# One product per tile for v and the router, selection in two halves, and written-out routed turns on TensorE: an attention block with routed experts on one core

## The chip, the cores and the metric

The kernel runs on one NeuronCore of a Trainium2 chip. The metric is the device time of one execution in microseconds. Every figure of the kernel before comes from one profiled execution of 688.34 us; three timed runs gave 687.27, 690.47 (the median) and 694.31 us. In the profile PE is TensorE (PEld its weight loads, PEldq its sequencer's own register and wait instructions), DVE is VectorE, ACT is ScalarE, POOL is GpSimd and SP is SyncE, which only issues DMAs here; a q behind an engine's name is its queue of such issues.

## The reference, cut to what matters

B=8 sequences of S=256 tokens with E=256 features, so T=2048 tokens or NT=16 tiles of 128.

```python
xn = layernorm(x)
# attention: 16 heads of 16, rope on q and k, causal
q, k, v = xn @ Wq + bq, xn @ Wk + bk, xn @ Wv + bv
attn = softmax(causal(rope(q) @ rope(k).T / sqrt(16))) @ v @ Wo + bo
# feed-forward: 64 experts of width 176, top 6 of a softmax, 2 shared experts
scores = softmax(xn @ gate_w.T)
topk_w, topk_ids = top_k(scores, 6)
topk_w = topk_w / (sum(topk_w) + 1e-20)
routed = sum over the six of topk_w * (silu(g) * u) @ w_down.T
shared = (silu(sg) * su) @ ws_down.T
return x + attn + routed + shared
```

## The kernel before, in words

The program is one block in which each engine has its own list of instructions and meets the others at semaphores (`then_inc` raises one, `wait_ge` waits for it). There are four stages, in this order on TensorE.

**Prologue.** DVE normalises the 16 tiles in four groups of 2, 2, 4 and 8 (`layernorm`, L700 to L719): statistics, an ACT square root (L537), two Newton steps, then one L718 per tile. TensorE begins with 20 idle products (`WARM`, L1022), then turns each tile over (`xn_transpose`, L1009), ACT copies it to `xnT` (L527), TensorE multiplies it by the 64 router columns (`route`, L1017), and ACT copies the logits (L532). The v products come apart from that, two tiles to a product (L1040): two of them after tile 3, two after tile 7, four among the q and k products. q and k are 16 products of 512 tokens (L1035), evacuated by ACT (L545). Meanwhile DVE picks the six experts of each token (L737 to L760) over all 16 tiles in one go: softmax, the eight largest (`max`), a mask of what lies above the sixth, and a scan that settles ties. TensorE waits for it at L1078, forms ranks from triangular products (L1083, L1084) and sends counts to DVE, which works out each slot's row and the tables of experts (L770 to L813). `tables_ok` lets TensorE go on into the shared experts.

**Shared experts** (32 tiles, L1148 to L1186), with DVE listing tokens beside them.

**Routed experts.** 128 tiles of 128 rows, each of two strips of 64 rows that may belong to different experts. Two tiles make a turn. In a turn TensorE does, in order: two `x_transpose` (L1135) of tiles four ahead, two `h_transpose` (L1171), two `up` (L1162) of tiles two ahead, two `down` (L1204). The first strip's weights are taken from a ring of eight experts at an address that is computed from a register; the second strip's weights are copied by DVE to a fixed place (`up_copy` L882, `down_copy` L888; `gu_own` and `dn_own` tell TensorE). After each `down` TensorE loads the expert number of the tile four ahead from the table in SBUF into a register (`load_expert`, L1111, a TENSOR_LOAD; DVE has its own, L872). All engines but POOL run most of the turns in a hardware loop of two turns (`eng.Fori`, L308), so the semaphore counts they wait for are computed from the loop register. `up` also waits for the ring's weights itself (`wait_weights`, L283 to L286). POOL gathers the tokens' rows (L442) and works through the rope of q and k beside that (`piece`, L445 to L481), eight pieces in all, each ending with eight DMAs of 256 KB (L455).

```python
def up(i, u):                                   # L1152
    pe.wait_ge(xgT_ok, i - SHARED_TILES + 1)
    pe.wait_ge(hid_ok, i - 1)
    wait_weights(pe, e)
    pe.wait_ge(gu_own, i - SHARED_TILES + 1)
```

**Attention** (64 pairs of heads, and the gathering of each token's six results).

## Time and profile before

| what | value |
|---|---|
| profiled execution | 688.34 us, of which the span from the first to the last instruction is 686.5 |
| three runs | 687.27, 690.47, 694.31 us |
| prologue, until the first shared product | 77.9 us |
| shared experts | 80.8 us |
| routed experts, from the first `up` to the last one | 357.3 us |
| the last `down`s and attention | 170.5 us |
| PE busy | 648.3 us (94%) |
| DVE, ACT, POOL busy | 447.3, 321.5, 360.9 us |

How to read it: the span is divided by what TensorE does, and a stage's idle time is its length less the busy time of PE in it. A busy PE can still be slow: its granted clock is full in all but a stretch of the prologue. The stages come one after the other on TensorE, so what one of them gives back shortens the whole, as long as nothing else was late at its end.

### The profile page before, as it was taken

The numbers are of one execution on the slowest core, as the hardware profiler recorded it, in microseconds if no ns is written. First come the engines' busy times: TensorE is split into PE (matmuls) and PEld (weight loads), VectorE is DVE, ScalarE is ACT, GpSimd is POOL, SyncE is SP. The second block draws the span as 40 slices with busy tenths as digits, with TensorE's granted clock in tenths as the row PEclk, the third lists the DMA queues.
The fourth block names the chain that finished last, engine by engine and source line by source line (L and its number), as shares of the span: only waits on it lengthen the run. The fifth ranks groups of instructions, "written<-read, shape, count | busy, mean of one in ns | idle before, by whom it ended". The sixth has DMA issues, their size and how long they took to land.

```text
span 686.5 us, 19625 instructions
## 1 busy us (share of the span) xinstructions
PE 648.3 (94%) x5132; PEld 398.5 (58%) x5133; DVE 447.3 (65%) x1331; ACT 321.5 (47%) x840; POOL 360.9 (53%) x376
## 2 busy tenths in 40 slices
PE   6999999999999899999989999999999899999997
PEld 3755677775455455555555555555554566666664
DVE  4568999997545464555546454554445699888864
ACT  2463323224444344443444354344446577676652
POOL 3000000028878586877868687785410576666662
PEclk9899999999999999999999999999999999999999
DMA  8250001126787878888796978887423777777432
GB/s 258 70 150 0 1 0 32 33 64 176 245 261 215 248 227 284 256 269 236 212 318 198 306 221 281 264 264 196 97 71 126 223 225 223 222 218 221 140 101 77
DMA packets 77139, 124.06 MB, mean 181 GB/s; under 512 B 11063, under 2 KB 51192, under 8 KB 77096
## 3 DMA queue, kind: packets, MB, share of 16 engines
q1 hardware_dynamic: 42376, 60.45, 28.3%
q0 software_dynamic: 15872, 46.16, 23.8%
q10 hardware_dynamic: 18848, 16.92, 7.3%
q8 instruction: 23, 0.38, 0.2%
q14 instruction: 20, 0.16, 0.1%
HBM read 85.73 MB, written 37.75 MB: 180 GB/s over the span
## 4 chain that ended last, share of the span: by engine, by line
PE 73%; DVE 9%; DMA 7%; issue 5%; ACT 2%; SPq 2%; DVEq 1%; POOL 1%; ACTq 0%; POOLq 0%
PE pair L1162 22%; PE pair L1204 12%; DMA lower<-wdn 6%; PE pair L1148 4%; PE pair L1035 4%; PE bank L1267 3%; PE bank L1171 3%; PE pair L1135 3%; PE pair L1186 3%; PE bank L1299 2%; PE pair L1040 2%; DVE space L862 2%; DVE negm L921 2%; PE pair L1222 2%; PE pair L1241 1%
## 5 line engine op out<-in xcount | busy, mean ns | idle before, releaser
L442 POOL DMA_INDIRECT lower<-xn_rows,idx_all x128 | 134.0, 1047 | 215.2 <-DVE idx_all L834 125.3
L1162 PE MATMUL pair<-space,work 128*64 (+1 forms) x768 | 167.9, 467 | 10.2 <-issue 3.4
L1204 PE MATMUL pair<-lower,work 88*64 x512 | 123.2, 380 | 2.1 <-ACT lower L607 0.8
L1162 PEld LDWEIGHTS pair<-space,work 128*64 128x64 f32 x768 | 66.9, 137 | 84.8 <-issue 55.6
L844 DVE TENSOR_TENSOR work<-work,pair 128x176 f32<-128x176 f32 x160 | 53.1, 336 | 95.1 <-ACT work L600 92.8
L600 ACT ACTIVATE work<-pair 128x176 f32<-128x176 f32 x160 | 51.1, 320 | 124.8 <-PE pair L1162 69.3
L1204 PEld LDWEIGHTS pair<-lower,work 88*64 88x64 f32 x512 | 69.0, 136 | 50.9 <-issue 11.7
L1162 PE MATMUL pair<-wqkv_sb,work 128*64 128x352 f32 x256 | 90.6, 477 | 0.0
L607 ACT ACTIVATE lower<-pair 128x256 f32<-128x256 f32 x128 | 49.2, 384 | 78.6 <-PE pair L1204 78.6
L507 POOL DMA_INDIRECT wqkv_sb<-y_rows,slot_i x48 | 47.1, 982 | 60.9 <-DVE negm L921 34.1
L921 DVE TENSOR_REDUCE negm<-pair 128x2 f32<-128x256 f32 (+1 forms) x128 | 65.0, 551 | 11.1 <-PE pair L1230 10.0
L647 ACT ACTIVATE pT<-pair 128x768 f32<-128x768 f32 x64 | 51.9, 812 | 42.8 <-PE pair L1253 41.4
L882 DVE COPY wqkv_sb<-space 128x704 f32 x64 | 49.6, 775 | 34.2 <-DMA lower<-wdn 19.9
L593 ACT ACTIVATE work<-pair 128x256 f32<-128x256 f32 x128 | 42.1, 381 | 54.0 <-PE pair L1135 34.7
L1204 PE MATMUL pair<-space,work 88*64 88x256 f32 x256 | 66.2, 381 | 0.0
L1204 PE MATMUL pair<-wqkv_sb,work 88*64 88x256 f32 x256 | 65.9, 379 | 0.0
L888 DVE COPY space<-lower 88x512 f32 x64 | 34.0, 532 | 34.4 <-issue 33.6
L507 POOL DMA_INDIRECT space<-y_rows,slot_i x48 | 45.8, 955 | 18.6 <-DVE x_all L965 9.7
L615 ACT ACTIVATE work<-bank 88x256 f32<-88x256 f32 x160 | 53.9, 383 | 2.0 <-PE bank L1171 2.0
L1171 PE MATMUL bank<-id_f,work 128*88 128x128 f32 x320 | 51.0, 273 | 0.7 <-DVE work L844 0.5
L882 DVE COPY space<-space 128x704 f32 x64 | 46.2, 723 | 8.1 <-issue 4.2
L1135 PE MATMUL pair<-id_f,lower 128*128 128x128 f32 x256 | 42.0, 286 | 6.8 <-issue 6.6
(186 smaller groups left out, 1219.2 us busy)
## 6 DMA issues: line engine op xcount, KB each, us to landing
space<-wgu SPq DMA_DIRECT2D x66, 352.0 KB
y_rows<-lower ACTq DMA_DIRECT2D x128, 128.0 KB
qk_all<-qk_rows SPq DMA_DIRECT2D x64, 256.0 KB, 4.2
lower<-wdn SPq DMA_DIRECT2D x66, 176.0 KB
qk_rows<-space POOLq DMA_DIRECT2D x32, 256.0 KB, 4.6
qk_rows<-qk_all POOLq DMA_DIRECT2D x32, 256.0 KB, 4.9
xn_rows<-qk_all SPq DMA_DIRECT2D x16, 128.0 KB, 1.9
lower<-xn_rows,idx_all POOLq DMA_INDIRECT x128
```

The lines of the kernel that those rows point to most:

```text
L442: po.indirect_dma_start(xg[:, r % XB, :], None, xn_rows[:, :], bass.IndirectOffsetOnAxis(idx_all[:, r:r + 1], 0)).then_inc(xg_in[r % XB], 16)
L507: po.indirect_dma_start(yg[u][:, k, :], None, y_rows[:, :], bass.IndirectOffsetOnAxis(slot_i[:, t, k:k + 1], 0)).then_inc(yg_in[u], 16)
L600: act.activation(sg[:, u % 2], pair[u % 2][:, 0:F], ACT.Silu).then_inc(silu_ok, 1)
L615: act.activation(hT[:, u % 2], bank[2 + u % 2][0:FP, 0:2 * P].rearrange("p (c t) -> p c t", c=2), ACT.Copy).then_inc(hT_ok, 1)
L647: act.activation(pT[:, n % G], pair[1][:].rearrange("p (j k) -> p j k", j=2)[:, :, 0:SPAN], ACT.Exp).then_inc(exp_done, 1)
L844: dve.tensor_tensor(hid[:, u % 2], sg[:, u % 2], pair[u % 2][:, F:2 * F], ALU.mult).then_inc(hid_ok, 1)
L882: dve.tensor_copy(own_gu[u % 2], wgu_sb[:, bass.ds((e + FIRST) % WB, 1)].rearrange("p o c n -> p (o c) n")).then_inc(gu_own, 1)
L921: last = dve.tensor_reduce(negm[:, qt, m % PAIRS_OF_HEADS], scores[:, :, qt * P:(2 * qt + 1) * P], AX.X, ALU.max, negate=True)
L1135: last = pe.transpose(bank[u % 2][:, c * P:(c + 1) * P], xg[:, u, c * P:(c + 1) * P], id_f[:])
L1162: last = pe.matmul(pair[u % 2][strip, 0:2 * F], xgT[u][:, c, strip], n, start=c == 0, stop=c == EC - 1, skip_group_check=True)
L1171: last = pe.transpose(bank[2 + u % 2][0:FP, c * P:(c + 1) * P], hid[:, u % 2, c * FP:(c + 1) * FP], id_f[:])
L1204: last = pe.matmul(pair[u % 2][strip, 512:512 + E], hT[:, u % 2, c, strip], n, start=c == 0, stop=c == 1, skip_group_check=True)
```

## The change

TensorE's idle products go from 20 to 9. The v columns and the router columns lie side by side in SBUF, and each tile has one product of 320 columns for both (`mix`), whose two results ACT copies apart; the eight v products are gone. The loads of the v and router weights go out on ACT's queue, behind the identity matrix. The norms have five groups, and the statistics of the next group's first two tiles stand ahead of a group's Newton steps, which wait for ACT's root. The selection runs over tiles 0 to 7 and then 8 to 15. It takes no softmax: it subtracts the maximum, takes the exponential (ACT: after tile 13's copy, and again ahead of the q and k products), finds the eight largest with `max`, overwrites the seventh and eighth, replaces each of the six once in a copy by -1 (`match_replace`, which finds one place for each), and takes what is below zero. The sum over all experts, needed for the small term in the divisor, is worked out later. TensorE forms the ranks of the first half after the third q/k product and those of the second half after the sixth. In the routed stage TensorE's loop is written out, so that its counts are constants, and `up` no longer waits for the ring's weights itself: DVE's copy, which it still waits for, has waited for them. The loops of DVE, ACT and SP stay.

```diff
-WARM = 20
+WARM = 9
+RANKS_AT = (2, 5)
-LN_GROUPS = ((0, 2), (2, 4), (4, 8), (8, 16))
+LN_GROUPS = ((0, 2), (2, 4), (4, 8), (8, 12), (12, 16))
+ROOT_AT = {1: 1, 3: 2, 6: 3, 9: 4}
+EXP_AT = 13
-        wqkv_sb = sb("wqkv_sb", [P, EC, 3 * E])
-        wr_sb = sb("wr_sb", [P, EC, NE])
+        wqkv_sb = sb("wqkv_sb", [P, EC, 3 * E + NE])
...
-            sp.dma_start(wqkv_sb[:, :, QK:], w[:, :, QK:]).then_inc(wv_in, 16)
...
-            act.dma_start(wr_sb[:], wr.rearrange("(c p) n -> p c n", p=P)).then_inc(wr_in, 16)
+            act.dma_start(wqkv_sb[:, :, QK:3 * E], wqkv.rearrange("(c p) n -> p c n", p=P)[:, :, QK:]).then_inc(wv_in, 16)
+            act.dma_start(wqkv_sb[:, :, 3 * E:], wr.rearrange("(c p) n -> p c n", p=P)).then_inc(wv_in, 16)
...
             for t in range(NT + 1):
                 if t < NT:
                     xnT_copy(t)
-                if t and t not in V_AFTER:
-                    logits(t - 1)
+                if t in ROOT_AT:
+                    root(ROOT_AT[t])
+                if t == EXP_AT:
+                    exponentials(0)
+                if t:
+                    logits(t - 1)
+                    v_copy(t - 1)
...
             for g, (t0, t1) in enumerate(LN_GROUPS):
-                layernorm(g, t0, t1)
+                link(moments(t0 + (2 if g >= 2 else 0), t1))
+                variances(t0, t1)
+                if 1 <= g < len(LN_GROUPS) - 1:
+                    moments(t1, t1 + 2)
+                normed(g, t0, t1)
...
+            for h in range(2):
+                t0, t1 = HALF * h, HALF * (h + 1)
+                p, c = prob[:, t0:t1], col[:, t0:t1]
+                dve.wait_ge(logit_ok, t1)
+                link(dve.tensor_reduce(c, p, AX.X, ALU.max, negate=True))
+                dve.tensor_tensor(p, p, c.unsqueeze(2).to_broadcast([P, HALF, NE]), ALU.add).then_inc(exp_in, 1)
...
+                dve.wait_ge(exp_ok, h + 1)
+                for t in range(t0, t1):
+                    last = dve.max(top[:, t], prob[:, t])
+                link(last)
+                link(dve.memset(top[:, t0:t1, TOPK:8], ABSENT))
+                for t in range(t0, t1):
+                    last = dve.match_replace(tmp[:, t], top[:, t], probs[:, t], TAKEN)
+                link(last)
+                link(dve.tensor_scalar(sel_b[:, t0:t1], tmp[:, t0:t1, 0:NE], 0.0, None, ALU.is_lt))
+                for t in range(t0, t1):
+                    link(dve.tensor_tensor(run_b[:, t + 1], run_b[:, t], sel_b[:, t], ALU.add))
+                dve.sem_inc(chosen, 1)
...
+            def mix(t):
                 pe.wait_ge(xnT_ok, t + 1)
+                if t >= 4:
+                    pe.wait_ge(v_ok, t - 3)
                 for c in range(EC):
+                    last = pe.matmul(half_bank[t % 4][:, 0:E + NE], xnT[:, t, c], wqkv_sb[:, c, QK:], start=c == 0, stop=c == EC - 1)
+                last.then_inc(mixed, 1)
...
                 pe.wait_ge(xgT_ok, i - SHARED_TILES + 1)
                 pe.wait_ge(hid_ok, i - 1)
-                wait_weights(pe, e)
                 pe.wait_ge(gu_own, i - SHARED_TILES + 1)
...
-            experts([(AHEAD_X, x_transpose), (0, h_transpose), (2, up), (0, down)], pe)
+            for i in range(SHARED_TILES - 2, TILES, 2):
+                for lead, do in ((AHEAD_X, x_transpose), (0, h_transpose), (2, up), (0, down)):
+                    for n in (i + lead, i + lead + 1):
+                        if SHARED_TILES + (AHEAD_X if lead == AHEAD_X else 0) <= n < TILES:
+                            do(n, n % XB)
```

First place: TensorE at the start of the prologue. Of before, from the idle products to the second pair of v products; `wr_sb` holds the router's weights, `wqkv_sb` those of q, k and v, `space` the turned tiles.

```order
L1022 MATMUL pair<-ones_b 128x512 x20
L1009 MATMUL pair<-id_f,qk_all 128x128 x4
L1017 MATMUL bank<-wr_sb,space 128x64 x2
L1009 MATMUL pair<-id_f,qk_all 128x128 x2
L1017 MATMUL bank<-wr_sb,space 128x64 x2
L1009 MATMUL pair<-id_f,qk_all 128x128 x2
L1017 MATMUL bank<-wr_sb,space 128x64 x4
L1050 MATMUL pair<-id_f,bqk_sb 128x1 x4
L1040 MATMUL pair<-wqkv_sb,space 128x256 x8
```

The same place in the changed kernel.

```order
L1019 MATMUL pair<-ones_b 128x512 x9
L1006 MATMUL pair<-id_f,qk_all 128x128 x4
L1014 MATMUL pair<-wqkv_sb,space 128x320 x2
L1006 MATMUL pair<-id_f,qk_all 128x128 x2
L1014 MATMUL pair<-wqkv_sb,space 128x320 x2
```

The v products have moved into the tiles' own products, and the bias products (L1050) stand after the last tile now.

Second place: DVE's selection. Of before, from the maximum over all 16 tiles to the running counts `run_b`.

```order
L737 TENSOR_REDUCE col<-space 128x16
L738 TENSOR_TENSOR space<-space,col 128x1024
L740 TENSOR_REDUCE col<-space 128x16
L741 RECIPROCAL col<-col 128x16
L742 TENSOR_TENSOR space<-space,col 128x1024
L745 MAX top<-space 128x8 x16
L748 TENSOR_TENSOR space<-space,top 128x1024
L749 TENSOR_REDUCE col<-space 128x16
L750 TENSOR_SCALAR col<-col 128x16
L751 TENSOR_TENSOR lower<-space,top 128x1024
L753 SCALAR_TENSOR_TENSOR space<-lower 128x64 x16
L755 TENSOR_TENSOR space<-space,col 128x1024
```

In the changed kernel, the whole of one half.

```order
L749 TENSOR_REDUCE col<-space 128x8
L750 TENSOR_TENSOR space<-space,col 128x8x64
L755 MAX top<-space 128x8 x8
L757 MEMSET top 128x8x2
L759 MATCH_REPLACE lower<-top,space 128x66 x8
L761 TENSOR_SCALAR sel_b<-lower 128x512
L763 TENSOR_TENSOR run_b<-run_b,sel_b 128x64 x8
```

Seven kinds of instruction per half stand where before fifteen did for the whole; the normalisation, the tie scan and the products of masks are gone.

Third place: TensorE in a routed turn, the first strip pair of `up` and the end of a `down`. Of before, inside the loop.

```order
L285 REGISTER_ALU [waits hid_ok,xgT_ok]
L285 ISA
L286 ISA [waits w_loaded_even]
L1162 ISA [waits gu_own,w_loaded_odd]
L1162 MATMUL pair<-space,work 64x352
L1162 MATMUL pair<-wqkv_sb,work 64x352
```

```order
L1198 REGISTER_ALU [waits hT_ok]
L1199 REGISTER_ALU [waits y_ok]
L1204 REGISTER_ALU [waits dn_own]
L1204 ISA
L1204 MATMUL pair<-lower,work 64x256
```

The same in the changed kernel.

```order
L1143 REGISTER_ALU [waits gu_own,hid_ok,xgT_ok]
L1143 ISA
L1143 MATMUL pair<-space,work 64x352
L1143 MATMUL pair<-wqkv_sb,work 64x352
```

```order
L1185 REGISTER_ALU [waits dn_own,y_ok,hT_ok]
L1185 ISA
L1185 MATMUL pair<-lower,work 64x256
```

The arithmetic for the counts (L285, L286, L1198, L1199) and both waits for the ring's weights are gone; the address that is worked out from the expert's register behind the wait for `gu_own` stays, and so does the TENSOR_LOAD after each `down`.

## Rows read from the trace of the kernel before

**Rows 1.** The page: busy time of each engine and its share of the span.

```profile
PE 648.3 (94%) x5132; PEld 398.5 (58%) x5133; DVE 447.3 (65%) x1331; ACT 321.5 (47%) x840; POOL 360.9 (53%) x376
```

**Rows 2.** Windows by stage: stretch, length, busy per engine, PEclk, DMA share, GB/s.

```profile
0.00:77.92 77.92, 70.60 (x280) 43.55 (x282) 51.50 (x191) 31.63 (x69) 5.98 (x16) 0.96 0.35 106
...
158.72:516.05 357.33, 338.17 (x2502) 192.06 (x2501) 189.43 (x377) 158.64 (x498) 255.34 (x258) 1.00 0.76 231
516.05:686.50 170.45, 159.37 (x1930) 104.48 (x1929) 131.89 (x337) 107.57 (x197) 92.95 (x96) 1.00 0.60 179
```

**Rows 3.** Timeline of PE in the prologue: start, length, line, shapes, count.

```profile
3.79 6.92 PE L1022 MATMUL pair<-ones_b 128*128 128x512 bf16 x20 [3.79 <-DMA id_f<-ident]
...
27.06 3.67 PE L1040 MATMUL pair<-wqkv_sb,space 128*128 128x256 f32 x16
...
35.82 0.39 PE L1009 MATMUL pair<-id_f,qk_all 128*128 128x128 f32 x2
...
39.62 20.88 PE L1035 MATMUL pair<-space,wqkv_sb 128*128 128x512 f32 x48
...
77.75 2.53 PE L1148 MATMUL pair<-space 128*128 128x352 f32 x8
```

**Rows 4.** Windows around the stretch of lower clock (columns as in rows 2).

```profile
11.00:13.00 2.00, 0.81 (x6) 0.52 (x4) 0.48 (x3) 0.94 (x4) 0.00 (x0) 1.00 1.12 326
...
17.00:22.00 5.00, 5.00 (x15) 4.10 (x15) 4.93 (x21) 0.89 (x3) 0.60 (x3) 0.50 0.32 107
```

**Rows 5.** Timeline of DVE in the prologue: norms and selection.

```profile
6.26 0.74 DVE L718 TENSOR_SCALAR qk_all<-x_all,mv,rstd 128x256 f32<-128x256 f32 x2
...
45.38 2.13 DVE L745 MAX8 top<-space 128x8 f32<-128x64 f32 x16
...
51.52 3.02 DVE L753 TENSOR_TENSOR_SCAN space<-lower 128x64 f32<-128x64 f32 x16
...
59.09 3.59 DVE L760 TENSOR_TENSOR run_b<-run_b,sel_b 128x64 bf16<-128x64 bf16 x16
```

**Rows 6.** Timeline of PE: the first `up` product of five turns (162.99 to 511.23 us).

```profile
162.99 0.51 PE L1162 MATMUL pair<-space,work 128*64 x1 [0.47 <-DVE space L882]
...
421.33 0.51 PE L1162 MATMUL pair<-space,work 128*64 x1
...
428.21 0.51 PE L1162 MATMUL pair<-space,work 128*64 x1 [0.37 <-issue]
...
433.48 0.51 PE L1162 MATMUL pair<-space,work 128*64 x1
...
511.23 0.51 PE L1162 MATMUL pair<-space,work 128*64 x1
```

**Rows 7.** Instructions by line on the sequencers: ns min/median/max, first to last start.

```profile
L1155 PEldq EVENT_SEMAPHORE  x119: 51/51/51, 179.1 to 515.2; - x119
L1157 PEldq EVENT_SEMAPHORE  x119: 51/51/51, 179.6 to 515.7; - x119
L308 PEldq COMPARE_BRANCH  x30: 76/208/243, 184.6 to 514.7; - x30
L1111 PEldq TENSOR_LOAD <-tile_e x120: 297/303/2263, 176.1 to 514.2; - x120
L872 DVEq TENSOR_LOAD <-tile_e x118: 299/498/2374, 179.0 to 511.8; - x118
```

**Rows 8.** Timeline of DVE and PE in two slow turns.

```profile
358.21 1.30 DVE L882 COPY wqkv_sb<-space 128x704 f32 x1 [0.73 <-DMA lower<-wdn]
359.44 0.51 DVE L882 COPY space<-space 128x704 f32 x1
...
359.84 0.51 PE L1162 MATMUL pair<-space,work 128*64 x1 [0.33 <-DMA lower<-wdn]
...
425.56 0.53 DVE L882 COPY wqkv_sb<-space 128x704 f32 x1 [0.67 <-DMA lower<-wdn]
```

**Rows 9.** DMA queues from 516 us on: packets, MB, share.

```profile
q8 instruction: 15, 0.25, 0.6%
```

More of the change, by code:

```diff
@@ L539, in projected @@
             def projected(n):
[L540 removed]
+                g, k = order[n]
                 act.wait_ge(proj_ok, n + 1)
[L542 to L549 removed]
+                if g == SPANS // 2 and k == 0:
+                    act.wait_ge(xn_out, 16 * NT)
+                act.activation(qT[:, g, k // 2, k % 2], projected_at(n), ACT.Identity, bias=bias_t[:, k // 2, k % 2:k % 2 + 1]
+                               ).then_inc(qkv_ok, 1)
             act.wait_ge(ones_ok, 1)
@@ L578, in _ @@
             act.wait_ge(hone_ok, 1)
-            act.wait_ge(exp_in, 1)
-            act.activation(prob[:], prob[:], ACT.Exp).then_inc(exp_ok, 1)
+            exponentials(1)
             act.activation(rstd[:, 0:1], var[:, 0:1], ACT.Silu)
             act.wait_ge(bias_ok, 1)
-            for n in range(NT // 4, len(order)):
+            for n in range(len(order)):
                 projected(n)
@@ L1056, in _ @@
                 if t < NT:
                     xn_transpose(t)
-                if t and t not in V_AFTER:
-                    route(t - 1)
+                if t == 1:
+                    pe.wait_ge(wv_in, 32)
+                if t:
+                    mix(t - 1)
+            pe.wait_ge(c_in_act, 16 * CONSTS)
+            for k in range(4):
+                last = pe.matmul(bank[2][:, k:k + 1], bqk_sb[:, k // 2 * E + k % 2:(k // 2 + 1) * E:2],
+                                 id_f[:, 0:1], start=True, stop=True)
@@ L1072, in _ @@
             pe.wait_ge(w_in, 16)
-            at_plan = 17
-            for n in range(NT // 4, at_plan):
-                project(n)
-            pe.wait_ge(consts_b, 1)
-            pe.wait_ge(chosen, 1)
-            pe.wait_ge(ones_ok, 1)
-            for h in range(2):
-                o = bank[h][:]
-                t0, t1 = NT // 2 * h, NT // 2 * (h + 1)
-                pe.matmul(o, tri_b[:], sel_b[:, t0:t1].rearrange("p t e -> p (t e)"), start=True, stop=False)
-                pe.matmul(o, ones_b[:], run_b[:, t0:t1].rearrange("p t e -> p (t e)"), start=False, stop=True)
@@ L1093, in _, with project @@
-            project(at_plan + 2)
-            project(at_plan + 3)
-            pe.wait_ge(passed_ok, 1)
-            pe.matmul(bank[2][0:1, P:P + STRIPS * RT], ones_c[:], passed[:].rearrange("p g i -> p (g i)"), start=True, stop=True
-                      ).then_inc(ended, 1)
-            for n in range(at_plan + 4, len(order)):
-                project(n)
+            def project(n):
+                g, k = order[n]
+                if n < 4:
+                    pe.wait_ge(v_ok, NT - 3 + n)
+                else:
+                    pe.wait_ge(qkv_ok, n - 3)
+                for c in range(EC):
+                    last = pe.matmul(projected_at(n), wqkv_sb[:, c, k // 2 * E + k % 2:(k // 2 + 1) * E:2],
+                                     xnT[:, g * (SPAN_T // P):(g + 1) * (SPAN_T // P), c], start=c == 0, stop=c == EC - 1)
+                last.then_inc(proj_ok, 1)
@@ new lines, in ranks @@
+            def ranks(h):
+                pe.wait_ge(chosen, h + 1)
+                t0, t1 = HALF * h, HALF * (h + 1)
+                pe.matmul(bank[h], tri_b[:], sel_b[:, t0:t1].rearrange("p t e -> p (t e)"), start=True, stop=False)
+                pe.matmul(bank[h], ones_b[:], run_b[:, t0:t1].rearrange("p t e -> p (t e)"), start=False, stop=True)
+            for n in range(len(order)):
+                project(n)
+                if n == RANKS_AT[0]:
+                    pe.wait_ge(consts_b, 1)
+                    pe.wait_ge(tables_in, 1)
+                    ranks(0)
+                if n == RANKS_AT[1]:
+                    ranks(1)
+                    pe.wait_ge(bias_ok, 1)
+                    pe.matmul(bank[2][0:NE, 0:1], run_b[:, NT], ones_b[:, 0:1], start=True, stop=True).then_inc(counted, 1)
+                if n == RANKS_AT[1] + 1:
+                    pe.wait_ge(tiled, 1)
+                    pe.wait_ge(row_ok, 1)
+                    pe.matmul(bank[3][:, 0:NE], ntile_b[:], before_sb[:], start=True, stop=True)
+                    pe.matmul(bank[2][0:NE, 1:2], upto_sb[:], ntile[:], start=True, stop=True)
+                    pe.matmul(bank[2][0:1, 64:64 + NE], ntile[:], upto_sb[:], start=True, stop=True).then_inc(placed, 1)
+                if n == RANKS_AT[1] + 4:
+                    pe.wait_ge(passed_ok, 1)
+                    pe.matmul(bank[2][0:1, P:P + STRIPS * RT], ones_c[:], passed[:].rearrange("p g i -> p (g i)"), start=True,
+                              stop=True).then_inc(ended, 1)
```

181 lines of the change are left out of this document (52 added, 129 removed).

## The prediction

> **What bounds the kernel now.** I read the page first: of a span of 686.5 us PE is busy for 648.3, 94% [rows 1], so only time in which PE idles, runs slowly or does work that can go is to be had. The windows by stage come next [rows 2]: the prologue lasts 77.92 us with 70.60 busy, the routed stage 357.33 with 338.17. The change touches these two. The other two it leaves as they are, and I carry their lengths over.
>
> In the prologue PE's timeline shows three things [rows 3]: 20 idle products until 10.7 us, though DVE has the first two normalised tiles by 7.0 (6.26 + 0.74) [rows 5]; a q/k stretch that begins at 39.62; and the first shared product at 77.75. The clock is part of it: granted 0.50, the lower level (1.2 GHz), from 17 to 22 us, after a stretch (11 to 13 us) in which PE was busy for 0.81 of 2 us [rows 4].
>
> In the routed stage I took the start of the first `up` product of every turn. From 162.99 to 511.23 there are 61 turns in 348.24 us [rows 6], 5.71 each. 16 of them take 5.27 or 5.28, as 428.21 to 433.48; in those PE works without a gap, so that is the floor of the matrix work. 61 floors are 321.5, and 26.8 us are excess. 13 turns longer than 5.8 hold 18.0 of it, as 421.33 to 428.21 (6.88); the other 48 hold 8.8.
>
> What makes them long stands in the sequencer's rows. PE's TENSOR_LOAD takes 303 ns in the median but up to 2263, DVE's 498 and up to 2374 [rows 7]; the long ones lie in the turns in which POOL has just issued its 256 KB DMAs, and PE's sequencer takes nothing else up meanwhile. Outside of them the sequencer is no more than some tenths of a microsecond ahead of the array: from one wait of an `up` (L1155) to the next (L1157) it takes 0.5 us, the first and the last of 119 alike [rows 7], two tiles a turn. So a long load becomes a gap on the array. The other limit is DVE: a copy of 1.30 us (its neighbour of the same shape took 0.51) ended at 359.51 and PE began at 359.84 [rows 8], 0.33 behind it.
>
> **The change part by part.**
>
> *Start.* 9 idle products end between 6.9 us (the mean of 0.346 in rows 3) and 7.7 (0.43, the pace of the first ones, worked out below), so PE meets the first tiles at about 7.6. The pace: 20 products take 6.92; a product of 512 bf16 columns needs 0.213 at 2.4 GHz and 0.427 at 1.2, so some 12 ran at the lower level. Both `mix` waits and the root of the next group then stand in ACT's and DVE's order: the second group's tiles come at 10.3 to 11.0 us (13.6 now), the third group's at 14.6. PE waits about 1.5 us twice, in place of a run of idle products.
>
> *One product per tile.* 256 columns take 0.229 a pass (3.67/16), 512 take 0.435 (20.88/48) [rows 3]; 320 lie at 0.28 between. Four passes are 1.12, a tile's turning 0.25 (0.39 for two, overlapped), so 1.35 to 1.4 a tile at full clock. ACT has three copies of a tile, by my estimate 1.0 in all, and keeps up. From the fifth tile at 14.6 the rest takes 12 x 1.35 plus the fourth tile's 1.1, and, as an estimate, 0.75 for ACT's detour to its first exponential: 32.7 us. If the clock stays at the lower level for as long as it does now (6.6 us), half of that, 3.3, comes on top: 36.0.
>
> *Up to the shared experts.* Bias, rope tables and bias row take 3.5, as now; 16 q/k products of 1.735 (four passes of rows 3) 27.8; ranks and counts 2.1. That is 33.4 us, all on PE: 66.1 or 69.4, against 77.92. The gain is 11.9 or 8.6; I take 10. The v products that stood among the q/k products (four of 1.7) make up 6.9 of it.
>
> *Selection.* It must not be late. `match_replace` is not in this trace. Its nearest rows are the MAX8 (2.13/16 = 0.13) and the scan (3.02/16 = 0.19) [rows 5]; with 0.13 to 0.38 (two scans) a half takes 1.07 for MAX8, 1.1 to 3.0, 0.6 for the mask and 1.8 for the counts (half of 3.59), so 4.6 to 6.5. I take 5. The second half then ends 9.5 to 11.5 us behind the mixing, and PE comes for it at 14.3 (3.5 + 6 x 1.735 + 0.4): no wait. DVE's remaining tables end at 28, PE's products at 33.4. So all that DVE saves here is covered by PE and counts for nothing, and if that cover went the first 5 us would still be free. The moved loads of the v and router weights (320 KB ahead of x) delay x by about 1 us at the 326 GB/s of the start [rows 4]; that is in the 11.0 above.
>
> *Written-out turns.* Per turn the sequencer loses two times 0.45 us of waits and arithmetic in `up` [rows 7], about 0.3 in the two `down`s, and half of a loop's end (0.21 for the branch and 0.1 around it): 1.3 to 1.5 of 5.0. The array's work is the same. What this gives back is worked out turn by turn: the new turn is the longer of 5.27 and the end of DVE's first copy plus 0.34. Over the 61 turns that makes 327.0 against 348.2, a gain of 21.3: 16.0 in the 13 long turns (two loads of some 1.0 us over the usual are then covered by the 1.4), 5.3 in the others. Left over are 5.5 us in which DVE's copy is the limit. From the 21.3 I take 4 away: DVE's own long loads stay, and with PE no longer late they come to the front at about 0.3 us in each long turn. So 17; bounds 3 (only the turns without a long load gain, and part of that) and 21.
>
> *Code.* Written out, the routed turns are fetched once instead of looped. In the last stretch, written out already, PE runs 1930 products and as many loads [rows 2] and its queue fetched 15 packets [rows 9], one per 257. A turn has some 112 instructions, so 64 turns need 28 packets, one per 12 us as there; no gap of PE in that stretch is put down to it. I count 0.
>
> The Trainium skill, page "Runtime: NRT & Kernel Launch", section "Instruction fetch mechanics", says that an engine fetches its next block while it runs the present one, and that a taken branch is what breaks this. By that the written-out stage costs nothing and the loop's branch goes; the trace agrees as far as the 15 packets without a gap go.
>
> The sum against the profiled execution: 688.34 - 10 - 17 = 661.3. The median of the runs was 2.1 above that execution, within their spread of 7. I forecast 662 us.
>
> **The rivals.**
>
> *DVE holds the turn.* DVE has two TENSOR_LOADs a turn as well, a longer median (498 ns), and its loop stays. If its late copies, not PE's sequencer, end the long turns, then only the small gaps go. For it: the slow turn of rows 8, where PE began 0.33 behind the copy. Against it: in the 6.88 turn DVE's copy had ended at 426.09 [rows 8] and PE began at 428.21 [rows 6], 2.1 us later. Gain 10 + 4: 674 us.
>
> *The clock stays low in the prologue.* With 11 idle products fewer and two waits of 1.5 us, PE may be at 0.50 from 7.6 to 22 us rather than for 6.6: another 3.5 to 4, and mixing ends at 40, so the prologue gains 4 to 5. For it: the fall after 11 to 13 us [rows 4]. Against it: each tile now brings 1.12 us of product where it brought 0.56. 688.3 - 4.5 - 17: 667 us.
>
> The Trainium skill, "TensorE: Matmul & The Clock Gate", section "The HAM clock gate", speaks against fewer idle products: the array is throttled by default and only sustained activity releases it. The rows agree in that some 12 products ran slowly first.
>
> *Slower: the code is fetched late.* The routed stage is the one in which DMAs are thick (231 GB/s over it [rows 2]), and small reads took up to 2.26 us there [rows 7]. If each of the 28 fetches stalled PE by x, the time would be 661 + 28x; from x = 1.0 the change is lost. At 2.26 it is 725 us. For it: the long loads show that a read can be late. Against it: the last stretch has 179 GB/s [rows 2], nearly as much, and no such gaps.
>
> **How the numbers follow.** Forecast (655 to 668): 0.63. DVE holds the turn (668 to 678): 0.18. The clock: 0.14, inside 662 to 671. Late code: 0.05, of which 0.03 is slower. The range of 8 in 10 is 652 to 676: the low end is both terms at their best (11.9 + 21.3 gives 655) with 3 for the spread of the runs, the high end the first rival and 2. Runs of this kernel spread over 1%, so 1% (7 us) is what a measurement can tell. Faster by more than that: 0.94; within it: 0.03; slower: 0.03.
>
> **What would show it.** In the changed kernel's profile: the first `up_shared` product between 65 and 70 us; the first `mix` near 8.5, PE back to back from 15; no wait of PE for `chosen`. From the first to the last `up` 336 to 345 us in place of 357; the TENSOR_LOADs as long as now at worst, but the turns around them below 6 us; the gap before the first `up` of a turn gone, except where DVE's copy ended 0.3 us before. The prediction is wrong if turns of 6.7 us remain (DVE, or the loads themselves), if gaps of PE appear at every 250th instruction or so (code), or if the clock shows 0.50 beyond 20 us.

## The result and the profile after

The changed kernel takes 670.82 us (median of 4 runs, 669.88 to 671.05) against 692.12 us of the kernel before in the same comparison (687.27 to 694.31): ratio 0.970, 95% interval 0.964 to 0.976. It is faster, 9 us above the forecast of 662 and inside the range of 652 to 676; 670.8 lies in the band that was given to the rival *DVE holds the turn* (668 to 678), not in the forecast's own (655 to 668). The profiled execution took 671.05 us, 17.3 less than the profiled one of before, where the forecast's sum had 27.

The page of the changed kernel, to lay beside [rows 1]; the second line counts the packets in which instructions were fetched over the whole run, 23 before; the last line is the chain that ended last, which was 73% PE before:

```profile
PE 637.7 (95%) x5056; PEld 385.4 (58%) x5057; DVE 435.3 (65%) x1350; ACT 318.4 (48%) x850; POOL 362.1 (54%) x376
...
q8 instruction: 46, 0.75, 0.5%
...
PE 85%; DVE 7%; issue 3%; ACT 3%; DMA 2%; SPq 0%; DVEq 0%; ACTq 0%
```

The windows by stage, columns as in [rows 2]:

```profile
0.00:65.76 65.76, 60.06 (x203) 32.47 (x205) 45.29 (x215) 30.43 (x79) 6.36 (x16) 1.00 0.41 125
...
146.71:499.10 352.39, 337.89 (x2502) 189.74 (x2502) 184.93 (x376) 157.07 (x498) 256.37 (x258) 1.00 0.78 235
499.10:669.20 170.10, 159.43 (x1929) 104.52 (x1929) 131.93 (x337) 107.19 (x196) 92.75 (x96) 1.00 0.60 179
```

This is the whole account: the prologue is 12.0 us shorter (first `up_shared` product at 65.76 instead of 77.75 us), the shared stage as long as it was (81.0), the routed stage only 4.9 us shorter (352.4 for 357.3), the rest 0.3. PE's busy time in the routed stage hardly moved (337.9 for 338.2), so some 14.5 us of idle time are still in it.

PE in the new prologue, to lay beside [rows 3]:

```profile
3.94 4.02 PE L1019 MATMUL pair<-ones_b 128*128 128x512 bf16 x9 [3.94 <-DMA id_f<-ident]
...
8.96 1.69 PE L1014 MATMUL pair<-wqkv_sb,space 128*128 128x320 f32 x4
...
14.35 0.44 PE L1006 MATMUL pair<-id_f,qk_all 128*128 128x128 f32 x2 [0.91 <-DVE qk_all L712]
14.62 1.24 PE L1014 MATMUL pair<-wqkv_sb,space 128*128 128x320 f32 x4
15.71 0.38 PE L1006 MATMUL pair<-id_f,qk_all 128*128 128x128 f32 x2
15.92 1.24 PE L1014 MATMUL pair<-wqkv_sb,space 128*128 128x320 f32 x4
...
29.71 2.42 PE L1014 MATMUL pair<-wqkv_sb,space 128*128 128x320 f32 x8 [0.65 <-ACT space L519]
...
65.76 2.53 PE L1130 MATMUL pair<-space 128*128 128x352 f32 x8
```

From 14.62 to 15.92 a tile takes 1.30 us, and between 14.35 and 32.1 there is one gap, of 0.65, behind ACT's detour to the exponentials. The granted clock over the stretch that answers to [rows 4] stayed at the higher level:

```profile
17.00:22.00 5.00, 5.00 (x25) 3.66 (x24) 3.46 (x17) 3.28 (x14) 0.00 (x0) 1.00 0.32 106
```

VectorE's selection, second half, to lay beside [rows 5]:

```profile
36.66 1.11 DVE L755 MAX8 top<-space 128x8 f32<-128x64 f32 x8 [0.24 <-ACT space L533]
...
37.95 0.09 DVE L759 MATCH_VALUE_LOAD lower<-top,space 128x8 f32 x1
38.03 0.21 DVE L759 MATCH_REPLACE8 lower<-top,space 128x66 f32<-128x66 f32 x1
...
40.11 1.78 DVE L763 TENSOR_TENSOR run_b<-run_b,sel_b 128x64 bf16<-128x64 bf16 x8
46.90 0.15 DVE L767 COPY cnt<-bank 64x1 f32<-64x1 f32 x1 [5.01 <-PE bank L1071]
```

A half takes 5.2 us, is done at 41.9, and VectorE then waits 5.0 us for PE.

In the routed stage I took the turns as before, from the first `up` product of one to that of the next. 61 of them now take 343.6 us (348.2 before), 22.2 above 61 floors of 5.27 (26.8 before). Turns above 5.8 us: 12, which hold 16.4 (13 with 18.0 before). So the long turns are there as they were, up to 8.72 us. The register loads are, too; by line, to lay beside [rows 7] (count, and ns min/median/max):

```profile
L1093 PEldq TENSOR_LOAD <-tile_e x124: 294/302/2028, 153.3 to 496.9; - x124
...
L869 DVEq TENSOR_LOAD <-tile_e x124: 299/465/2734, 150.8 to 494.8; - x124
```

One long turn (7.18 us, from 209.51): the timeline of PE with ACT's copy of the hidden transposes, and the two loads of PE's sequencer in it.

```profile
209.51 0.51 PE L1143 MATMUL pair<-space,work 128*64 x1
...
210.76 0.66 ACT L605 ACTIVATE work<-bank 88x256 f32<-88x256 f32 x2
...
211.93 0.38 PE L1185 MATMUL pair<-lower,work 88*64 x1
...
213.34 0.42 PE L1185 MATMUL pair<-lower,work 88*64 x1 [0.38 <-issue]
...
215.69 0.63 PE L1117 MATMUL pair<-id_f,lower 128*128 128x128 f32 x4 [1.27 <-issue]
...
216.69 0.51 PE L1143 MATMUL pair<-space,work 128*64 x1
```

```profile
L1093 PEldq TENSOR_LOAD <-tile_e x2: 1202/1615/2028, 211.6 to 213.5; - x2
```

The first load starts at 211.6, when the `down` that it follows has been dispatched but has not begun on the array, and ends at 212.8, with 0.5 us of address arithmetic to come: the second `down` is late by 0.38. The second load, 2.03 us, begins at 213.5 and ends at 215.5; the array ran dry at 214.4. "Issue" is what such a gap is called: PE waited for nothing but its own sequencer.

One long turn in each of the two kernels has another cause. The granted clock falls to the lower level in the routed stage too, behind the longest turn. The windows of before, and of the changed kernel:

```profile
219.60:227.20 7.60, 5.62 (x40) 3.00 (x40) 2.69 (x8) 3.30 (x11) 3.48 (x5) 1.00 0.98 317
227.20:230.61 3.41, 3.24 (x12) 1.51 (x14) 0.47 (x2) 0.81 (x3) 3.10 (x5) 0.50 0.73 238
```

```profile
172.57:180.39 7.82, 5.29 (x38) 2.65 (x38) 3.48 (x9) 2.87 (x9) 6.91 (x9) 1.00 0.91 287
180.39:183.80 3.41, 3.41 (x16) 1.61 (x15) 0.00 (x0) 1.15 (x3) 2.88 (x4) 0.50 1.03 398
```

In the stretch before it PE was busy for 5.62 of 7.60 us and for 5.29 of 7.82. So the clock of the kernel before is not full outside the prologue, and the turn behind the longest one (6.85 us from 227.37 before, 6.50 from 181.29 now) is long by the clock and not by a load: 3.2 and 2.5 us of it lie in these stretches, and half of that, 1.6 and 1.3 us, is by this estimate its whole excess. e1 and e9 below have one such stretch in the routed stage, e2 two, the other kernels none.

### The profile page after: what moved, and what is told of

It reads as the page before. It is cut to its first block, busy times and chain, and to the rows that moved or that the text cites. A ratio compares the mean times of both kernels' runs of the same rounds, so it can differ in the third digit from the quotient of the medians.

```text
span 669.2 us, 18755 instructions
## 1 busy us (share of the span) xinstructions
PE 637.7 (95%) x5056; PEld 385.4 (58%) x5057; DVE 435.3 (65%) x1350; ACT 318.4 (48%) x850; POOL 362.1 (54%) x376
## 4 chain that ended last, share of the span: by engine, by line
PE 85%; DVE 7%; issue 3%; ACT 3%; DMA 2%; SPq 0%; DVEq 0%; ACTq 0%
PE pair L1143 24%; PE pair L1185 17%; PE pair L1117 5%; PE bank L1152 5%; PE pair L1130 4%; PE pair L1052 4%; PE bank L1252 4%; PE pair L1167 3%; PE bank L1284 2%; PE pair L1014 2%; DVE space L859 2%; PE pair L1207 2%; PE pair L1226 2%; DVE negm L918 2%; PE pair L1215 2%
## 5 line engine op out<-in xcount | busy, mean ns | idle before, releaser
L1143 PEld LDWEIGHTS pair<-space,work 128*64 128x64 f32 x768 | 66.1, 137 | 76.9 <-issue 61.9
L597 ACT ACTIVATE lower<-pair 128x256 f32<-128x256 f32 x128 | 49.1, 384 | 83.1 <-PE pair L1185 83.1
```

The lines of the kernel that those rows point to most:

```text
L1143: last = pe.matmul(pair[u % 2][strip, 0:2 * F], xgT[u][:, c, strip], n, start=c == 0, stop=c == EC - 1, skip_group_check=True)
```

## The experiments

The theory after this reading: the prologue gives its 12 us; the written-out turns take away small gaps, but not the long turns, which come from register loads (PE's and VectorE's) that are slow while GpSimd's q/k row writes run, and from VectorE's copies. Rivals: the written-out turns gain nothing, or gain 17 that something else takes back; late gathers and weights, not loads, make the long turns.

What the runs gave, in one table (stretch: first to last `up`, 63 turns; excess: 61 turns less 61 x 5.27; all from the timelines of one profiled execution; time: median of the runs):

| kernel | stretch | excess | turns over 6 us, their excess | time |
|---|---|---|---|---|
| before | 357.3 | 26.8 | 10, 16.2 | 688 to 692 |
| changed | 352.4 | 22.2 | 12, 16.4 | 670.8 |
| e1 changed, loop back | 360.0 | 29.4 | 11, 18.6 | 678.9 |
| e2 before, written out | 352.7 | 22.5 | 14, 17.3 | 683.2 |
| e3 no loads on PE | 346.0 | 15.2 | 8, 8.2 | 663.3 |
| e4 no loads on VectorE | 349.5 | 19.2 | 7, 10.1 | 668.5 |
| e5 no loads on both | 343.4 | 12.8 | 3, 4.5 | 662.2 |
| e6 writes spread | 347.7 | 17.5 | 13, 13.0 | 666.2 |
| e7 e5 and e6 | 342.5 | 11.9 | 4, 5.2 | 660.9 |
| e8 e5 without rope | 330.9 | 0.6 | 0 | 649.3 |
| e11 e5, rope paced | 338.2 | 6.2 | 0 | 656.9 |

Rows of one profile each are not sharp. The changed kernel, e2, e9, e10 and e12 run the same routed code, and their stretches are 352.4, 352.7, 350.0, 351.1 and 350.9 us, their excess 22.2, 22.5, 19.8, 21.0 and 20.6; before and e1 run the same loop, with 357.3 and 360.0. Two rows that differ by less than 3 us are not told apart by this table alone.

### e1 and e2: the two parts apart

e1 is the changed kernel with the loop and its wait:

```diff
+                wait_weights(pe, e)
...
-            for i in range(SHARED_TILES - 2, TILES, 2):
...
+            experts([(AHEAD_X, x_transpose), (0, h_transpose), (2, up), (0, down)], pe)
```

> TensorE's routed turns go back into the loop, with the wait for the weights; the new prologue stays. Theory (the two parts add up, and the written-out turns are the small one): the first up_shared stays near 65.8 us, the stretch from the first to the last up goes back from 352.4 to about 357 us, and the time is 5 to 9 us above the changed kernel, 676 to 680 us. Rival (the whole gain is the prologue's): the stretch stays at 352 and the time at 671 us. Rival (the prediction's size for the turns holds and something else took it back): the stretch grows by 10 or more, time 681 us or above.

e2 is the kernel before with the same lines the other way round.

> The kernel before with nothing changed but TensorE's routed turns, written out and without their wait for the weights. Theory: the stretch from the first to the last up is about 352 us instead of 357, the time 5 to 9 us under the kernel before. Rival (the prediction's size): stretch 340, time 17 us under the kernel before. Rival (the longer code costs something that the new prologue hides): no gain.

e1: 678.92 us (674.91 to 680.53), ratio to before 0.984 (0.979 to 0.990). e2: 683.19 us (681.16 to 685.82), ratio 0.991 (0.988 to 0.994). The routed stages of e1 and of e2:

```profile
146.51:506.49 359.98, 338.65 (x2501) 191.84 (x2501) 191.08 (x376) 157.46 (x498) 255.09 (x258) 1.00 0.77 229
```

```profile
157.86:510.52 352.66, 339.36 (x2501) 189.77 (x2501) 186.89 (x377) 156.85 (x498) 255.42 (x258) 0.99 0.78 235
```

The parts add up: against 689.05 us e1 gains 10.1 and e2 5.9, and the changed kernel gained 17 to 21. The written-out turns are worth 5 to 8 us of stretch, on the old prologue and on the new one, and 7.2 by the means of the two profiles with the loop (358.7) and the five without (351.4). The code is fetched with 47 packets in e2 and 23 in e1, and costs nothing that shows: e8 below, written out too and fetched with 47, leaves PE idle for 0.3 us in the whole routed stage.

### e3, e4, e5: no register loads in the routed stage

VectorE packs four expert numbers into a word, and each engine loads 32 words in the shared stage:

```diff
+            for k in range(2, -1, -1):
+                link(dve.scalar_tensor_tensor(tile_p[:], tile_e[:, :, 3::4] if k == 2 else tile_p[:], 7, tile_e[:, :, k::4],
+                                              ALU.logical_shift_left, ALU.bitwise_or))
...
-                pe.reg_load(expert_reg[u], tile_e[0:1, 0, bass.ds(i, 1)])
+                pe.reg_load(expert_reg[k], tile_p[0:1, 0, bass.ds(SHARED_TILES // 4 + k, 1)])
...
-                return pe.snap(expert_reg[u], min_val=0, max_val=XT - 1) & (P - 1)
...
+                r = i - SHARED_TILES
+                v = pe.snap(expert_reg[r // 4], min_val=0, max_val=(1 << 28) - 1)
+                return (v >> 7 * (r % 4)) & (P - 1)
```

e3 does it on PE, e4 on VectorE, e5 on both. In e4 and e5 VectorE's turns are written out for it, so what its loads cost and what its loop costs are not told apart.

> The changed kernel with no register load left in the routed stage: VectorE packs the expert numbers of four tiles into one word, TensorE and VectorE each load 32 such words in the shared stage, one per turn, and take a number out by a shift and a mask; VectorE's routed turns are written out too. Theory (the turns above 6 us that are left come from register loads of up to 2.7 us beside GpSimd's q/k row writes): of the 22.2 us by which 61 turns exceed 5.27 us, some 12 go, the stretch from the first to the last up falls from 352 to about 340 us, the time to 658 to 662 us. Rival (late gathers and weights, or copies slowed by GpSimd's rope, hold these turns): the stretch stays at 350 to 353 us and the time at 669 to 672 us. Under both, the 64 loads of 0.3 us in the shared stage hide, and it stays at 81 us; if not, it grows by up to 10 us.

> TensorE alone without register loads in the routed stage (32 packed words loaded in the shared stage); VectorE keeps its loads and its loop. The kernel with both packed had a stretch from the first to the last up of 343.4 us and 662.2 us of time. Theory (both engines' loads count, TensorE's more, since most of the gaps in the turns above 6 us begin behind its own loads): stretch 345 to 348 us, time 664 to 667 us. Rival (only VectorE's loads count, by late copies): stretch 351 to 353, time 670 to 672 us. Rival (only TensorE's count): 343 to 344 us and 662 us.

> VectorE alone without register loads in the routed stage, its turns written out; TensorE keeps its loads. Theory (both count, TensorE's more): stretch 348 to 351 us, time 667 to 670 us. Rival (only VectorE's count): stretch 343 to 344 us and 662 us. Rival (only TensorE's count): 352 us and 671 us.

e5: 662.17 us (660.82 to 663.87); e3: 663.25 (662.01 to 664.47); e4: 668.47 (668.01 to 669.29). The routed stages of e3, e4 and e5:

```profile
146.05:492.00 345.95, 335.34 (x2501) 189.44 (x2501) 191.53 (x376) 156.16 (x498) 253.82 (x258) 1.00 0.79 239
```

```profile
146.74:496.20 349.46, 337.03 (x2501) 188.51 (x2500) 191.10 (x378) 156.05 (x498) 249.90 (x258) 1.00 0.79 237
```

```profile
146.78:490.20 343.42, 334.42 (x2502) 189.92 (x2501) 188.79 (x378) 156.12 (x498) 249.53 (x258) 1.00 0.80 241
```

PE's loads held 7.0 us of the excess (22.2 to 15.2), VectorE's loads with its loop 3.0, both 9.4. The changed kernel's 22.2 include some 1.7 us lost to the lower clock (half of the 3.41 from 180.39) and 2.4 us of waiting for gathers in its longest turn; against e10 and e12, which have no low clock there, PE's loads are worth 5.8 and 5.4. PE's part is clear in the times, 663.3 against 669.0 to 670.9 for the four kernels with the changed kernel's loads. VectorE's part alone is not: e12 took 669.02 us and e4 668.47.

e5 falls 3 us short of what was expected of the stretch: its first two turns, 7.58 and 6.59 us, hold 3.6 of the 12.8 left. In them a VectorE copy takes 2.2 us.

Two readings fall with this. In the changed kernel six gaps of the second `down`, 4.6 us in all, are put down to ACT's y copy (L597), which had ended some tenths of a microsecond before. Two of them end 0.50 us behind a load on PE's sequencer, four 0.39 us behind VectorE's down copy, which began behind a VectorE load of 1.6 to 2.7 us and itself took 1.0 to 2.2. With PE's loads gone (e3) five such gaps are left, now all behind VectorE's copy; with VectorE's gone (e4) two are left, both behind a load of PE; in e5 there is none. And the longest turn, 8.72 us from 172.57, with PE waiting 0.98 and 1.46 us for gathers, has no counterpart in e3 to e5: there the turns near 170 are below 6 us. Why the gathers are then in time was not tried.

### e6 and e7: the writes spread

```diff
-            steps = [(n, k) for n in range(PIECES) for k in range(PIECE_STEPS)]
+            steps = []
+            for n in range(PIECES + 1):
+                for k in range(ROPE_STEPS):
+                    if n < PIECES:
+                        steps.append((n, k))
+                    if n and k < 2 * COPIES:
+                        steps.append((n - 1, ROPE_STEPS + k))
```

> The changed kernel with GpSimd's q/k row writes of one piece spread between the rope operations of the next piece, instead of eight in a row; the same writes in all. Theory (the writes in a row make the register loads long): the loads above 1 us become fewer, the turns above 6 us too, time 661 to 667 us. Rival (it is GpSimd's rope beside VectorE's copies that counts): each turn now has some rope operation beside its copies, and the time is 671 us or up to 5 us more.

e6: 666.16 us (664.80 to 668.54). Its loads by line, PE's and VectorE's:

```profile
L1099 PEldq TENSOR_LOAD <-tile_e x124: 295/301/976, 152.8 to 491.7; - x124
...
L875 DVEq TENSOR_LOAD <-tile_e x124: 298/491/2286, 150.2 to 489.5; - x124
```

PE's longest load falls from 2028 to 976 ns; over 300 ns each, its 124 loads cost 4.3 us in sum where they cost 19.2 (VectorE's 41.3 for 44.2). So the writes in a row are what makes PE's loads long. The trace of the changed kernel says the same: all 21 of PE's loads above 0.6 us run between the issue and the landing of such a write, and of the 76 loads that do not, none is above 0.6. VectorE's loads stayed long; what they wait for is open. One part of the theory missed: the turns above 6 us did not become fewer (13 for 12), only their excess fell (13.0 for 16.4).

> Both engines packed, and GpSimd's q/k row writes spread between the next piece's rope operations. Theory (the writes in a row hurt through the register loads alone, and what is left are VectorE's copies beside the rope): no further gain over both packed, stretch 341 to 345 us, time 660 to 664 us. Rival (the writes in a row also make weights and gathers late): stretch 336 to 339 us, time 655 to 658 us.

e7, with e5's packing, gives 660.91 us (660.78 to 661.39): with the loads gone, spreading the writes gains little more.

### e8: the rope left out

e8 is e5 with GpSimd's rope operations replaced by one-column copies, so queries and keys are left unrotated.

```diff
-                if k < 2:
-                    i = po.tensor_tensor(batches(other[:, k]), batches(q[:, 1 - k]), sin, ALU.mult)
...
+                if k == 0 and n < BUFS:
+                    i = po.memset(other, 0.0)
+                else:
+                    i = po.tensor_copy(other[:, k % 2, 0:1], q[:, k % 2, 0:1])
```

> Both engines packed, and GpSimd's rope left out: 72 operations of 128x512 or 128x1024 become a copy of one column each (four a fill of the buffer with zeros), so queries and keys are wrong; the writes of the q/k rows stay. Theory (what is left above 5.27 us a turn is VectorE's copies beside the rope, 0.5 us grown to 1.0 to 2.2): 61 turns come to 322 to 325 us, the stretch from the first to the last up to 331 to 334 us, time 650 to 653 us. Rival (the copies are late by themselves, by the weights' loads or the order of VectorE's turn): stretch 340 to 343 us, time 659 to 662 us.

649.28 us (648.87 to 650.32). The routed stage:

```profile
146.15:477.00 330.85, 330.55 (x2501) 189.51 (x2501) 154.17 (x378) 155.16 (x498) 173.35 (x258) 1.00 0.82 251
```

PE is busy for 330.55 of 330.85 us: 57 of the 61 turns are at the floor, and the excess is 0.6. VectorE does the same 378 instructions in 154.2 us that took it 188.8 in e5. What was left after the loads, 12.2 us, is VectorE beside GpSimd's rope. GpSimd issues the gathers too, but no gap of PE in e5's 61 turns ends with a gather, so an earlier gather is not what e8 gains. How it looks, in e5's timeline of GpSimd, VectorE and PE:

```profile
195.79 1.27 POOL L468 TENSOR_TENSOR qk_all<-qk_all,space 128x512 f32<-128x512 f32 x1 [0.18 <-POOL qk_all L466]
...
196.05 1.40 DVE L885 COPY wqkv_sb<-space 128x704 f32 x1 [0.46 <-DMA lower<-wdn]
...
197.22 1.11 POOL L470 CAST space<-qk_all 128x1024 fp32r<-128x1024 f32 x1 [0.17 <-POOL qk_all L468]
197.37 1.35 DVE L885 COPY space<-space 128x704 f32 x1
197.95 0.51 PE L1149 MATMUL pair<-space,work 128*64 x1 [0.34 <-issue]
```

Both copies (0.53 us alone) end 0.39 us behind the rope operation that was running when they began: 197.06 to 197.45, 198.33 to 198.72. So do all 42 copies of this shape in e5's routed stage that begin while a rope operation runs: they take 0.56 to 1.59 us and end 0.38 to 0.40 us behind it. In e8 all 126 copies of this shape take 0.53. The Trainium skill, page "SBUF — State Buffer", section "SBUF: two separate sides", says that VectorE and GpSimd share a pair of ports, which one of them locks for a whole instruction while the other waits. The trace agrees: however long a copy was held up, it ended the same time behind the rope operation, so it is not slower, it begins later.

### e11: the rope paced

```diff
...
+                if r >= 2 * XB + 1:
+                    po.wait_ge(dn_own, r - 2 * XB + 1)
+                while ropes and todo - len(ropes) < (r - XB + 1) * todo // (RT - 2 * XB):
+                    piece(*ropes.pop(0))
+                    if writes and (not ropes or writes[0][0] < ropes[0][0]):
+                        piece(*writes.pop(0))
```

> Both engines packed, and GpSimd's rope paced: about one operation a turn, begun when VectorE's two down copies of the turn are done, each followed by one write of the piece before. Theory (the 12 us left over both packed are copies slowed by rope that runs at the same time; beside VectorE's pause in a turn it costs little): of the 12.8 us by which 61 turns exceed 5.27 us 2 to 5 stay, the stretch from the first to the last up is 333 to 336 us, the time 651 to 655 us. Rival (the rope slows VectorE wherever it stands, by the hidden products too, or the wait holds up the gathers): stretch 341 us or more, time 659 us or more.

656.93 us (656.29 to 657.15), ratio to before 0.954 (0.950 to 0.958), 14 us below the changed kernel: the best of these kernels that leaves nothing out. The routed stage:

```profile
146.68:484.84 338.16, 331.51 (x2502) 190.88 (x2501) 169.60 (x378) 156.54 (x498) 251.19 (x258) 1.00 0.82 245
```

No turn is above 6 us and 48 of 61 are at the floor, but 6.2 us of excess stay, above the 2 to 5 expected, and stretch and time are 2 us above what was expected: in 13 turns an up copy still takes 1.3 to 1.8 us. 11 of the 13 are among the 12 turns that have a second rope operation by this schedule (72 in 60 turns).

### e9, e10 and e12: the prologue

```diff
-WARM = 9
+WARM = 20
```

for e9, and 2 for e10.

> The changed kernel with 20 idle products at its start, as before, instead of 9. Theory (in the changed kernel the mixing products begin as soon as the idle ones end, and the full clock was there with 9): the idle products end 4.9 us later, near 12.9 us, the wait for the third group of tiles at 14.35 us hides about 1 us of that, the first up_shared comes at 69 to 70 us instead of 65.8, the time is 674 to 675 us. Rival (the tiles' arrival sets the start): first up_shared 66 to 67 us, time 671 to 672 us.

> The changed kernel with 2 idle products instead of 9. Theory (the idle products are what gives the mixing its full clock): TensorE has little to do until 8.5 us, the granted clock shows 0.50 over some of the first 20 us, the mixing ends 2 to 4 us later, the first up_shared comes at 68 to 70 us, the time is 673 to 675 us. Rival (nine were more than needed, or the wait for tiles hides the slow start): first up_shared 65 to 66 us, time 670 to 672 us.

PE at the start of e9, and of e10 (the third mixing product of e10 is the one from 13.09):

```profile
3.78 6.82 PE L1019 MATMUL pair<-ones_b 128*128 128x512 bf16 x20 [3.78 <-DMA id_f<-ident]
...
11.38 1.31 PE L1014 MATMUL pair<-wqkv_sb,space 128*128 128x320 f32 x4 [0.35 <-ACT space L519]
...
16.69 0.44 PE L1006 MATMUL pair<-id_f,qk_all 128*128 128x128 f32 x2 [0.98 <-DVE qk_all L712]
```

```profile
7.99 2.47 PE L1014 MATMUL pair<-wqkv_sb,space 128*128 128x320 f32 x4
...
10.68 2.34 PE L1014 MATMUL pair<-wqkv_sb,space 128*128 128x320 f32 x4
...
13.09 1.24 PE L1014 MATMUL pair<-wqkv_sb,space 128*128 128x320 f32 x4
15.33 0.44 PE L1006 MATMUL pair<-id_f,qk_all 128*128 128x128 f32 x2 [1.00 <-DVE qk_all L712]
```

The windows of e10 in which its first two mixing products ran:

```profile
7.00:9.00 2.00, 1.86 (x6) 1.25 (x6) 1.90 (x9) 0.89 (x3) 0.00 (x0) 1.00 1.10 347
9.00:11.00 2.00, 2.00 (x6) 1.27 (x5) 1.86 (x8) 0.51 (x3) 0.00 (x0) 1.00 1.08 376
```

The first two products take twice the 1.24 us of the third, as was expected of the lower level, but the clock column shows 1.00. That 1.00 is no reading. The trace's records of the granted clock begin with its rise to the higher level, at 12.91 us in e10, 9.72 in the changed kernel and 8.74 in before, and a window without a record shows 1.00. So with 2 idle products PE was at the lower level until 12.91 us, with 9 until 9.72.

Both 670.94 us (669.22 to 673.57, and 669.56 to 671.55). In the stage the theory holds at a smaller size: the first `up_shared` comes at 68.1 us with 20 idle products and at 66.7 with 2, against 65.76 with 9. (The 20 ended at 10.60, not near 12.9 as expected, so the first `up_shared` moved by less.) In the time neither shows, as the routed stretch of the same routed code varies by more than that, from 350.0 to 352.7 us. So these two are inconclusive for the time. With 20, the third group of tiles came 2.3 us later (16.69 for 14.35): its root stands behind the copies of earlier tiles in ACT's order, and PE set the pace of those.

e12 does the second half's maxima and match-and-replace twice:

```diff
+                for _ in range(1 + h):
+                    for t in range(t0, t1):
+                        last = dve.match_replace(tmp[:, t], top[:, t], probs[:, t], TAKEN)
+                    link(last)
```

> The changed kernel with the second half's maxima and match-and-replace done twice, the same result, 2.8 us more on VectorE before TensorE's second ranks. Theory (VectorE's selection is covered by the q and k projections with 4 to 5 us to spare, so what the new selection saves is not in the time): chosen for the second half near 44.7 us instead of 41.9, TensorE does not wait there, the first up_shared stays at 65.8 us and the time at 670 to 672 us. Rival (VectorE's chain reaches the end of the prologue): 2 to 3 us more, 673 to 674 us.

669.02 us (667.93 to 669.12), not slower. VectorE's next instruction after the selection, in e12:

```profile
46.35 0.15 DVE L769 COPY cnt<-bank 64x1 f32<-64x1 f32 x1 [2.15 <-PE bank L1073]
```

It still waits 2.15 us for PE, where it waited 5.01. The 2.8 us went into its slack: what the new selection saves VectorE is covered by PE, as forecast.

## Why the prediction was right or wrong

*Start, and one product per tile: right.* The idle products ended at 7.96 (6.9 to 7.7 forecast, so 0.3 late), the third group came at 14.35 (14.6), PE waited 0.9 there and hardly at all for the second group (1.5 each forecast); a tile takes 1.30 us (1.35 to 1.4), the detour to the exponentials costs 0.65 (0.75), and mixing ended at 32.1 (32.7).

*Up to the shared experts: right, at the upper case.* 33.6 us for 33.4. The clock did not fall to 0.50 in the prologue, so the first `up_shared` came at 65.76 (66.1 in that case). The 10 taken between the two cases measured 12.0. The rival with a clock that stays low is out. (The clock does show 0.50 beyond 20 us, which the forecast named as a sign of being wrong; but it does so in the routed stage, as it did before.) Which part of the change gave how much of the 12.0 was tried only for the idle products (2.3, e9) and the selection (nothing, e12).

*Selection: right.* A half took 5.2 us for 5; `match_replace` starts every 0.20 us, in the range of 0.13 to 0.38. PE never waits for it, and e12 shows the slack.

*Written-out turns: the step that failed.* The term of 17 measured 4.9 in the two profiles, 5.9 in e2's time, and 7.6 between the stretches of e1 and the changed kernel. The step is "two loads of some 1.0 us over the usual are then covered by the 1.4": 16.0 were to come back in the 13 long turns, and 1.6 did (18.0 to 16.4); over all profiles of either code the long turns hold 18.0 to 21.1 with the loop and 15.5 to 17.3 without. The 5.3 in the other turns measured 3.0.

The forecast took the time freed in the sequencer as a lead that it could run up before a load. It cannot: PE's first load of a turn stands behind a `down`, which waits for the hidden transposes. In the turn at 209.51 ACT's copy for the first `down` ended at 211.15, PE's sequencer had stood idle for 0.9 us by then, and the load began at 211.6. The lead at a load, from its start to the end of the `down` ahead of it on the array, was 1.3 us at that turn's first load and 0.9 at the second. Over the 61 turns its median is 1.45 us at the first load and 1.13 at the second before, 1.51 and 1.38 in the changed kernel: 0.06 and 0.25 more, where 1.4 a turn was counted on. What became of the rest stands in the records of PE's sequencer: its gaps of over 0.15 us that end with the release of a semaphore add up to 94 us over the 61 turns, 15 before: 57 are behind VectorE's up copy (8.5 before), 32 behind ACT's copy of the hidden transposes (3.0 before). The written-out sequencer reaches its waits earlier and stands there. No run took one of these waits away; that the loads hold the turns is shown by e3 and e5.

The forecast's own test, turns of 6.7 us that remain "(DVE, or the loads themselves)", came out against it three times (8.72, 7.24, 7.18 us). And its 13 long turns had one that no load made, the one from 227.37 at the lower clock.

*DVE holds the turn.* The rival's gain of 4 is near what was measured, but its mechanism holds only part of it: VectorE's loads with its loop are worth 2.4 (e3 to e5) or 3.0 us (to e4), which is not clear of the spread, PE's 5 to 7. The larger part of VectorE's share has another cause, its copies beside the rope, which the forecast put at 5.5 us and e8 shows to be 12.2 once the loads are gone.

*Code: right.* 46 packets for 23, and by e8 no gap.

*The sum.* 688.3 less 12.0, 4.9 and 0.3 is 671.1, the profiled time. The forecast is off by 2 one way in the prologue and by 12 the other way in the routed stage. That the time still lies inside the range is owed to the rival *DVE holds the turn*, which set the range's upper end, and not to the mechanism of the written-out turns.

## What to carry to other kernels

Time freed in an engine's instruction stream helped here only up to the next semaphore wait; to judge whether it covers a slow instruction, look at how far ahead of the array that instruction is reached, not at how much was saved per turn. Small register loads inside a steady loop are better packed and done in a stage that has slack (9 us here), and work for GpSimd is better timed to VectorE's pauses than merely off the critical path (5 us here). A gap's named releaser that had ended well before the gap did is a sign that something else came last. And before a turn's excess is put down to one cause, its clock is to be looked at.

## What the runs showed of the hardware that was not expected

- A register load on PE goes from 0.3 to 2 us while the q/k row writes run, and PE's (not VectorE's) shrink to below 1 us when the same writes are spread.
- A 128x704 copy on VectorE, 0.53 us alone, takes up to 2.2 us beside GpSimd's tensor operations, and every copy of over 0.6 us in e5's routed stage ends 0.38 to 0.40 us behind such an operation; the whole routed stage costs VectorE 34.6 us more for them.
- The granted clock fell to the lower level in the routed stage behind a turn in which PE was busy for 5.29 of 7.82 us (5.62 of 7.60 before), and the next turn was 1.3 us longer for it (1.6 before).
- In e10 two products took 2.47 and 2.34 us where the same product takes 1.24: they ran ahead of the first record of the clock, where its column shows 1.00 without one. There a known product's duration tells the level.
